# Another split of rounding and bias over the engines in the first attention layer of a four-layer network

## The reference

```python
q = (x @ Wq + bq).reshape(1, B * N, H, hd)          # x: layer-normed, B = 8, N = 128, H = 16, hd = 16
kv = (cond @ Wkv + bkv).reshape(1, -1, 2, H, hd)    # all 8 batches together: 1024 keys
q, k = _fq_sym(q / 4, axis=-1), _fq_sym(k, axis=-1) # rounded to 8-bit steps, per head and token
v = _fq_sym(v, axis=2)
attn = softmax(einsum('bhqd,bhkd->bhqk', q, k))
attn = _fq_unsigned(attn, axis=-1)                  # s = max / 255; round(attn / s) * s
x = x + einsum('bhqk,bhkd->bhqd', attn, v).reshape(B, N, C) @ Wp + bp
```

## Time and profile before

| | before |
|---|---|
| median of 3 executions | 2335.09 us (2330.97 to 2339.15) |
| the profiled execution | 2333.09 us, span from first to last instruction 2331.3 us |
| the head loop in it | about 93 to 357 us |
| busy over the span | PE 1749.9, DVE 1245.6, ACT 849.2, POOL 714.1 us |
| DVE maxima (L1754) | 128 of 1217 ns |
| ACT exponentials (L1734) | 128 of 1204 ns, and 128 accumulator reads of 191 ns |
| POOL biases (L1675) | 128 of 615 ns |

### The profile page before, as it was taken

How to read it: one execution, slowest core, us unless ns; L and a number is a source line. 1 busy time by engine, 2 the same in 40 slices (tenths; PEclk the granted TensorE clock), 3 DMA queues, 4 the chain that set the end, 5 groups by cost and what they waited for, 6 DMA issues and landing times. The chain is left out here.

```text
span 2331.3 us, 28461 instructions
## 1 busy us (share of the span) xinstructions
PE 1749.9 (75%) x8489; PEld 1094.2 (47%) x8492; DVE 1245.6 (53%) x2738; ACT 849.2 (36%) x2046; POOL 714.1 (31%) x1414
## 2 busy tenths in 40 slices
PE   5677764998783599991698989888499878726663
PEld 4322223555452355551355556556255566525442
DVE  4889982223553422227577878778322345652222
ACT  1866661111221111112366666667211144402221
POOL 0123320000100000005777788776000020007884
PEclk8655555999686699995799999999699978857887
DMA  1277771110003111102000000000111000066866
GB/s 61 47 130 137 131 129 46 34 40 20 1 1 145 39 52 58 58 30 64 10 1 0 0 0 0 0 0 0 31 34 34 20 27 0 0 242 155 205 137 144
DMA packets 180391, 132.09 MB, mean 57 GB/s; under 512 B 141986, under 2 KB 163490, under 8 KB 177235
## 3 DMA queue, kind: packets, MB, share of 16 engines
q1 hardware_dynamic: 160370, 104.40, 17.1%
q0 software_dynamic: 12976, 20.46, 4.8%
q10 hardware_dynamic: 6960, 6.19, 0.8%
HBM read 81.62 MB, written 15.83 MB: 42 GB/s over the span
## 5 line engine op out<-in xcount | busy, mean ns | idle before, releaser
L1327 PE MATMUL l2x_pr<-l_w,l2x_xs 128*128 128x512 f32 x512 | 250.2, 614 | 81.2 <-POOL l2x_xs L1285 81.2
L1734 ACT ACTIVATE l0m_pf<-l0m_s,l0m_bias,l0x_sq 128x1024 f32<-128x1024 f32 x128 | 154.1, 1204 | 86.2 <-POOL l0m_bias L1675 86.1
L1754 DVE TENSOR_REDUCE l0m_mx<-l0m_s 128x1 f32<-128x1024 f32 x128 | 155.6, 1217 | 34.1 <-PE l0m_s L1687 33.9
L259 PE MATMUL l1e_gu<-x_normT,l1e_w 128*128 128x512 f32 x384 | 170.8, 598 | 3.2 <-DMA l1e_w<-in_l_ffn 3.0
L1327 PEld LDWEIGHTS l2x_pr<-l_w,l2x_xs 128*128 128x128 f32 x512 | 93.2, 195 | 156.3 <-issue 151.1
L1675 POOL TENSOR_SCALAR l0m_bias<-l0m_mx,l0x_nsq 128x1 f32<-128x1 f32 x128 | 78.7, 615 | 266.6 <-DVE l0m_mx L1754 265.2
L1687 PE MATMUL l0m_s<-l0x_kT,l0x_qT 48*128 48x512 bf16 x256 | 131.6, 618 | 6.9 <-PEq L1499 4.1
L1451 DVE TENSOR_SCALAR l2x_raw<-l2x_raw,l2x_mv,l2x_rs 128x128 f32<-128x128 f32 x384 | 128.0, 396 | 15.2 <-POOL l2x_rs L1306 15.2
L300 DVE TENSOR_TENSOR l1e_h<-l1e_sil,l1e_gu 128x512 f32<-128x512 f32 x48 | 33.0, 688 | 182.5 <-ACT l1e_sil L285 169.8
L1441 DVE BATCH_NORM_STATS2 l2x_bn<-l2x_raw 128x6 f32<-128x128 f32 x384 | 83.3, 278 | 86.5 <-ACT l2x_raw L1390 86.4
L259 PE MATMUL l0e_gu<-x_normT,l0e_w 128*128 128x512 f32 x272 | 121.3, 600 | 9.0 <-DMA l0e_w<-in_l_ffn 9.0
(11 more groups left out here) (465 smaller groups left out, 3988.7 us busy)
## 6 DMA issues: line engine op xcount, KB each, us to landing
l3m_w<-in_l_moe SPq DMA_DIRECT2D x16, 1280.0 KB, 7.4
l1e_w<-in_l_ffn SPq DMA_DIRECT2D x24, 384.0 KB, 2.9
l_w<-in_l_w SPq DMA_DIRECT2D x4, 2048.0 KB, 14.8
l0e_w<-in_l_ffn SPq DMA_DIRECT2D x17, 384.0 KB, 3.0
l2e_w<-in_l_ffn SPq DMA_DIRECT2D x16, 384.0 KB, 2.9
l1e_route<-l_route SPq DMA_DIRECT2D x8, 512.0 KB
l2q_wps<-in_l_wp SPq DMA_DIRECT2D x16, 256.0 KB, 2.6
l_w<-l_acc SPq DMA_DIRECT2D x16, 256.0 KB, 4.9
```

Of the source, the lines that this page charges most:

```text
L259: last = nc.tensor.matmul(gu[half][:, m, :], w[:, slot, (2 * k + m) * P:(2 * k + m + 1) * P], pg.xnT[:, k, half * HALF:(half + 1) * HALF], ...
L1327: last = nc.tensor.matmul(flat(pr[t % 2][:]), xs[:, side, src, k, :], w[:, k, (side * 8 + t) * W:(side * 8 + t + 1) * W], start=(k == 0), ...
L1734: nc.scalar.activation(pf[:, n % 4, :], s_ps[n % 3][:], ACT.Exp, scale=sq[:, b, h:h + 1], bias=bias[:, n % 4:n % 4 + 1], accum_out=sm[:, b ...
L1754: nc.vector.tensor_reduce(mx[:, n % 4:n % 4 + 1], s_ps[n % 3][:], AX, ALU.max).then_inc(s["maxed"], 1)
```

## The change

Three things change in the head loop. Every fourth head (n % 4 == 3) is rounded by POOL instead of DVE, as soon as its exponential is done, with its own semaphore `pool_rounded`; SP, and ACT before it overwrites `pf`, wait for the one or the other by the number of the head. The bias is no longer computed by POOL but by ACT, as an Identity activation with scale `nsq` and bias `ln255` (a 128x1 tile that POOL sets once), right ahead of the exponential, which waits for it. The wait for the rounding of head n - 4 now stands ahead of the bias.

```diff
--- before.py
+++ after.py
@@ -1625,7 +1625,7 @@
 
                 ch.link(vec.tensor_tensor(pg.x[:], pg.x[:], bias[:, 2:3, :].to_broadcast([P, B, D]), ALU.add))
 
-        names = ("scores", "maxed", "biased", "exped", "rounded", "pv", "recip", "scaled", "o_turned", "o_kept", "out", "added")
+        names = ("scores", "logged", "maxed", "biased", "exped", "rounded", "pool_rounded", "pv", "recip", "scaled", "o_turned", "o_kept", "out", "added")
         s.update({m: pg.sem(f"l0x_{m}") for m in names})
         moved = [pg.sem(f"l0x_moved{i}") for i in range(4)]
         N, LAG = B * H, 5
@@ -1637,6 +1637,7 @@
                 return st.enter_context(nc.psum_tensor(f"l0m_{m}", shape, dt))
             mx = sb("mx", [P, 4])
             bias = sb("bias", [P, 4])
+            ln255 = sb("ln255", [P, 1])
             pf = sb("pf", [P, 4, T])
             pi = sb("pi", [P, 4, T], BF16)
             pT = sb("pT", [P, 4, B, P], BF16)
@@ -1653,6 +1654,18 @@
             SCALE, TURN, KEEP, OUT, ADD = H + LAG, H + LAG + 1, H + LAG + 1, H + LAG + 2, H + LAG + 3
             STEPS = N + LAG + 4
 
+            def wait_rounded(eng, n):
+                if n % 4 == 3:
+                    eng.wait_ge(s["pool_rounded"], n // 4 + 1)
+                else:
+                    eng.wait_ge(s["rounded"], n - n // 4 + 1)
+
+            def round_p(eng, n):
+                eng.wait_ge(s["exped"], n + 1)
+                if n >= 4:
+                    eng.wait_ge(moved[n % 4], 16 * (n // 4))
+                return pi[:, n % 4, :], pf[:, n % 4, :], ROUND, ROUND, ALU.add, ALU.subtract
+
             def due(n, at):
                 b, h = divmod(n - at, H)
                 return b if h == 0 and 0 <= b < B else None
@@ -1660,20 +1673,16 @@
             @block.sync
             def _(sp):
                 for n in range(N):
-                    sp.wait_ge(s["rounded"], n + 1)
+                    wait_rounded(sp, n)
                     if n >= 4:
                         sp.wait_ge(s["pv"], n - 3)
                     sp.dma_start_transpose(pT[:, n % 4], pi[:, n % 4, :]).then_inc(moved[n % 4], 16)
 
             @block.gpsimd
             def _(pool):
-                for n in range(N):
-                    b, h = divmod(n, H)
-                    pool.wait_ge(s["maxed"], n + 1)
-                    if n >= 4:
-                        pool.wait_ge(s["exped"], n - 3)
-                    nc.gpsimd.tensor_scalar(bias[:, n % 4:n % 4 + 1], mx[:, n % 4:n % 4 + 1], nsq[:, b, h:h + 1], float(np.log(255.0)),
-                                            ALU.mult, ALU.add).then_inc(s["biased"], 1)
+                nc.gpsimd.memset(ln255[:], float(np.log(255.0))).then_inc(s["logged"], 1)
+                for n in range(3, N, 4):
+                    nc.gpsimd.tensor_scalar(*round_p(pool, n)).then_inc(s["pool_rounded"], 1)
 
             @block.tensor
             def _(pe):
@@ -1726,9 +1735,12 @@
             def _(act):
                 def exps(n):
                     b, h = divmod(n, H)
+                    act.wait_ge(s["maxed"], n + 1)
+                    if n >= 4:
+                        wait_rounded(act, n - 4)
+                    nc.scalar.activation(bias[:, n % 4:n % 4 + 1], mx[:, n % 4:n % 4 + 1], ACT.Identity, scale=nsq[:, b, h:h + 1],
+                                         bias=ln255[:, 0:1]).then_inc(s["biased"], 1)
                     act.wait_ge(s["biased"], n + 1)
-                    if n >= 4:
-                        act.wait_ge(s["rounded"], n - 3)
                     if h == 0 and b >= 2:
                         act.wait_ge(s["scaled"], b - 1)
                     nc.scalar.activation(pf[:, n % 4, :], s_ps[n % 3][:], ACT.Exp, scale=sq[:, b, h:h + 1], bias=bias[:, n % 4:n % 4 + 1],
@@ -1739,6 +1751,7 @@
                     for k in range(KD):
                         nc.scalar.activation(oT[:, b % 2, k, :], f_ps[:, k * P:(k + 1) * P], ACT.Copy, scale=sv[:, k:k + 1]).then_inc(s["o_kept"], 1)
 
+                act.wait_ge(s["logged"], 1)
                 for n in range(STEPS):
                     if n < N:
                         exps(n)
@@ -1754,10 +1767,8 @@
                     nc.vector.tensor_reduce(mx[:, n % 4:n % 4 + 1], s_ps[n % 3][:], AX, ALU.max).then_inc(s["maxed"], 1)
 
                 def rounding(n):
-                    dve.wait_ge(s["exped"], n + 1)
-                    if n >= 4:
-                        dve.wait_ge(moved[n % 4], 16 * (n // 4))
-                    nc.vector.tensor_scalar(pi[:, n % 4, :], pf[:, n % 4, :], ROUND, ROUND, ALU.add, ALU.subtract).then_inc(s["rounded"], 1)
+                    if n % 4 != 3:
+                        nc.vector.tensor_scalar(*round_p(dve, n)).then_inc(s["rounded"], 1)
 
                 def scale(b):
                     dve.wait_ge(s["exped"], H * b + H)
```

## The result

| | before | after |
|---|---|---|
| median | 2337.91 us (20 executions) | 2345.18 us (20 executions) |
| ratio | 1 | 1.0035 [1.0024, 1.0047] |
| profiled execution, span | 2331.3 us | 2339.0 us |
| first scores to first exponential | 92.36 to 95.04: 2.7 us | 93.72 to 97.80: 4.1 us |
| first exponential to the end of the last | 253.5 us | 256.4 us |

The forecast was 2326 us, 9 us faster; the change made the kernel 7 us slower by the medians, 8 by the ratio. The three parts of the stage add up to 265.4 us before and 272.6 us after, 7.2 us more, and the spans differ by 7.7: the rest of the kernel kept its length within half a microsecond. So what follows is about the head loop alone.

The account below looks back on a forecast made before the run. DVE was taken to bound the head loop. Eight batches at 30.5 instead of 32.0 us save 12.0, the drain returns 2.2, leaving 9.8, rounded down to 9, off the median 2335.1: 2326 us; range 2317 to 2352.

Parts of the forecast that it names:

- The loop without lateness: Head loop: a batch along ACT takes 29.9 us instead of 32.0 if no POOL rounding is late.
- ACT as the next bound: Mid-batch: ACT becomes the bound at 1.66 us a head (bounds 1.48 to 1.75), ahead of DVE's 1.58.
- The batch-end chain: From the maximum before the batch-end stall to the one after it: 6.7 us instead of 6.92.
- The lateness: POOL's 2.84 us rounding makes head 17's maximum 0.6 us late, once a batch: 30.5 us instead of 29.9.
- My own formula: Head 11's exponential end at 8.0, then POOL's rounding, transpose, scores: head 17's maximum at 15.6 against 15.0, 0.6 us late.
- that far end: POOL's rounding at 4.0 us: batch 31.7 us, kernel 2334 us, upper end of the forecast's own range without blocking.
- The table load: Identity on ACT brings no table load; a rival had tables swapping, over 300 us slower (0.03 with the rest).
- The end: Drain after the loop: POOL rounds head 127 in 2.84 us instead of DVE's 0.69, 2.15 us more, uncovered.
- Rivals 1 and 2: Shared port shuts DVE out to POOL's end: 2336 us, chance 0.20; with a longer POOL rounding, 2352 to 2370, chance 0.20.
- Rival 2: POOL's rounding longer than 2.84 us blocks DVE at the shared port: 3.4 us gives 2352 us, 4.0 gives 2370; chance 0.20.
- Rival 3: POOL's rounding takes only 1.2 to 2 us: 16 us saved, 2319 us, chance 0.12.
- The list of signs: Expected in the profile: ACT's idle from 79.6 towards 25 us, DVE roundings at 0.68, maxima 1.66 apart, last transpose 2.2 later.

Follow-up runs that it names:

- the deep kernel: The changed kernel with eight buffers instead of four and the value product seven heads behind instead of five; 2324.1 us, ratio 0.994.
- the int16 kernel: The deep kernel without POOL rounding: ACT writes exponentials as int16, DVE casts them to bfloat16, table loaded before the first bias; 2312.68 us, ratio 0.9907.
- its deep version: The kernel before the change with eight buffers and the value product seven heads behind; 2334.61 us, ratio 0.9993.
- the bias-only kernel: The changed kernel with all 128 roundings back on DVE, only the bias moved to ACT; 2333.49 us, ratio 0.9985.
- the cast kernel: The changed kernel with a plain cast on POOL instead of the rounding for its 32 heads; 2326.28 us, ratio 0.9947.
- the operation aside: The bias-only kernel with POOL also executing the same rounding 32 times on tiles of its own that nobody waits for; 2353.28 us, ratio 1.0057.

## Why the prediction was wrong, step by step

The step that failed is the price of POOL's lateness: 0.6 us a batch, from a POOL operation of 2.84 us. The operation took 3.63 us and more, the stall 1.60 us, and lateness and port together 19.5 us where the forecast had 4.8. The forecast for the stage was 9.8 us less, and it became 7.2 us more: 17.0 us of error. By part of the stage:

| | forecast | measured | error |
|---|---|---|---|
| first scores to first exponential | 0 | +1.4 | 1.4 |
| loop | -12.0 | +2.9 | 14.9 |
| end | +2.2 | +2.9 | 0.7 |

- **The loop without lateness: right in size, in part by luck.** The forecast was 29.9 us a batch instead of 32.0, that is 16.8 us in all; the deep kernel, in which no rounding is late, shows 30.0 in most batches and a loop shorter by 253.5 - 236.9 = 16.6 us. But two errors cancel in it. With ACT's measured beat of 1.61 us and self-wait of 0.03 the sum gives 3.00 + 14 x 1.61 - 0.09 + 3.74 = 29.2 us, and the int16 kernel, where DVE is quick, shows 29.3. The 0.8 us between that and 30.0 is a term that I had left out: behind the batch-end stall DVE sets the pace for some heads. The exponentials of the deep kernel start there at 264.24, 266.30, 268.03 and 269.77, that is 2.06, 1.73 and 1.74 us apart, and only then 1.61. DVE as the bound before is confirmed by its deep version (no gain).
- **ACT as the next bound: right in kind.** The Identity took 0.380 us (forecast 0.37). Its self-wait is 0.03 us instead of 0.09, so ACT's beat is 1.61 us (288.54 behind 286.93), not 1.66, and DVE's 1.58 (6.33 us for four heads in the deep kernel) is almost level with it. The batch-end chain lost its 0.2 us and some more: DVE's stall there is 3.06 us in the bias-only kernel instead of 3.37, and its loop is 1.5 us shorter over eight batches.
- **The lateness: the term that failed.** The forecast had 0.6 us a batch, 4.8 in all; measured, after against deep, 256.4 - 236.9 = 19.5, port included. The place was right: it is the maximum of head 17 that is late, and it is late by 1.60 us. The size was not. I took 2.84 us from a row with one arithmetic operation; with two and a bfloat16 output it takes 3.63 us undisturbed, 3.90 for this head. My own formula with 3.90 gives 0.6 + 1.06 = 1.66 us, the trace 1.60. (It fits better than its terms deserve: the transpose lands after 2.7 us and not 3.1, which takes away 0.4, and ACT's quicker beat and POOL's start 0.08 us behind the exponential give about 0.3 back.) Such stalls come to 11.9 us over the loop. The range held 4.0 us, but as its far end and not as the likely value, although there was a second operation to do. And that far end was added up 2 us too low: 8 x 0.3 saved and 3.3 given back is 2336 us and not 2334. By its own sum, then, 4.0 us meant no change, so the length alone doesn't give the measured loss.
- **What I had at zero.** DVE's idle time before maxima, over the whole loop, is 26.6 us in the deep kernel and 40.6 in the changed one. Of these 14.0 us 11.9 are the stalls above, 2.8 a stall of 0.38 us (once 0.54) before the maximum of head 6, and 4.0 small ones, less 4.6 because the batch-end stall is 3.0 us long instead of 3.7. Roundings that meet POOL (722 against 693 ns) add 96 x 0.03 = 3 us; some 2.5 of the 19.5 us I can't place. "The next POOL head, 15, runs with the same lateness and adds none" is wrong at least in this, that it starts 0.4 us late for its own buffer. But the 0.38 us are not its doing: the cast kernel, where POOL is done sooner than DVE was, has the same stall. The scores of head 6 stand there behind the first value product of the new batch, which waits for DVE's scaling (1.25 us at 266.60 in the changed kernel). The 0.24 us follow a value product that waited 0.72 us for its transpose, landed 3.45 us after its issue. For the other small ones, depth removes buffer waits and transpose waits at once, and the runs don't tell them apart.
- **The table load: wrong for a reason that I had not looked at.** That Identity needs no load of its own is true, showed it, and there is still only one load. But the load of the exponential's table was hidden by being the first thing ACT did in the block, and the Identity took that place. I costed the load at nothing because none was added and did not ask what hid the old one. The Trainium skill (ScalarE: Activation LUTs, Table sets: the hidden batching unit) says that identity is in every set; the trace agrees, and it is just this that pushes the load behind the first bias. The same page of the Trainium skill (What ACT_TABLE_LOAD costs) gives 1283 ns for the load and 1380 more for a drain; here the load takes 1.28 us and the exponential starts 0.02 us behind it, so no drain is seen in this place.
- **The end: right in kind.** +2.9 us against 2.2: POOL takes 3.63 instead of 2.84, and starts 0.4 us late as in the loop; the quicker landing gives part of it back. The queue of transposes, which I let go with 1 us, is what kept it from shrinking by more than 1.1 us when the last head was DVE's.
- **Rivals 1 and 2, the shared port.** Neither is the main part of what happened: in the changed kernel the port costs DVE about 4 us, and adds 0.27 us to head 11's lateness. Rival 2 had the right cause, a longer POOL operation, by the wrong way: at 3.4 to 4.0 us it foresaw DVE kept out to POOL's end and 2352 to 2370 us. The time went its way because of late transposes; that it lies inside the range is luck. With the operation aside, the port did cost 13 us.
- **Rival 3, POOL is quick**: the cast, 1.04 us, shows that world: 0.9947, 12 us instead of the 16 it foresaw.
- **The list of signs.** ACT's idle was to fall to 25 us and stayed at 43: that alone said that ACT was not the bound. In the deep kernel it is 27. The mean of DVE's roundings, 722 ns, rightly showed a port that matters a little. The last transpose was to issue 2.2 us later behind the last exponential; POOL's end comes 4.1 us behind it instead of DVE's 0.7.

## What to carry to other kernels

Before work goes to a slower engine, measure that very instruction there (number of operations, output type), and follow its result to the end: here 0.6 us saved on DVE bought a result some 2 us later, and with four buffers in a ring its reader, the scores queued behind it and the next use of the buffer turned late. If an off-loaded step is late, give it depth before giving it up: the same split with eight buffers was 0.6% faster instead of 0.35% slower (with five it was only level, since DVE's roundings then fell on the end of POOL's operations). And when an instruction is put first on ACT, look what it displaces: a table load is free only while it stands under somebody else's wait.

## What the runs showed of the hardware

- A GpSimd TENSOR_SCALAR of 128x1024 float32 to bfloat16 with two immediates takes 3.63 us undisturbed, with one operation and float32 output 2.84, a plain cast to bfloat16 1.04 us. The Trainium skill (GPSIMD Engine Reference, Engine selection) has one-input operations at roughly line rate: the cast agrees, the TENSOR_SCALAR is 3.5 times slower.
- The port between DVE and GpSimd is not held for the whole instruction. In all seven kernels with this POOL operation, a DVE rounding that starts from 0.9 us behind POOL's start to 1.6 us before its end takes its plain 0.68 us (1.55 of 3.99, 2.68 of 4.25). One that starts 0.1 to 0.7 us behind POOL's start takes 0.87 to 1.44 us and ends 1.58 us behind that start. One that starts 1.0 to 0.2 us before POOL's end takes up to 1.54 us and ends 0.54 us behind that end (3.28 of 3.99, 2.94 of 3.64 and 2.91 of 3.63 take 1.24 to 1.26). POOL pays too: begun with 0.5 us of a DVE rounding still to run it takes 3.99 us instead of 3.63, and with a second rounding in its middle up to 4.34. The Trainium skill (SBUF — State Buffer, Who interferes with whom) says that whoever issues first keeps the pair for its whole instruction; that fits both ends of POOL's operation (there also the 0.79 us that DVE lost close behind its start) and not its middle.
- Transposes of 128x1024 bfloat16 queued on SP follow each other by 1.35 us. One lands 2.7 us after its issue in the median of the changed, the bias-only and the deep kernel, 3.1 in the kernel before and its deep version, and 3.3 in the int16 kernel; why is open.
- ACT writes int16 as fast as float32 (1.20 us for 1024 columns), the conversion takes the place of the separate rounding, and DVE casts int16 to bfloat16 in 0.42 us where the two-operation rounding from float32 takes 0.68.
